# Attention with two-bank maxima, an earlier turn of the maxima, the query copy on VectorE and one transpose of the biases

## The reference, cut to what matters

```python
xn  = layernorm(x)
q, k, v    = split(xn  @ Wqkv     + bqkv)        # 16 heads of 8
_, ka, va  = split(ctx @ Wqkv_aux + bqkv_aux)
p, pa = softmax(q @ k.T / sqrt(8)), softmax(q @ ka.T / sqrt(8))
out   = (p @ v) * (1 - gate) + (pa @ va) * gate
x     = x + tanh(g_xattn) * (out @ Wo + bo)
x     = x + tanh(g_ffn) * moe(layernorm(x))
```

## Time and profile before

| what | value |
|---|---|
| median of three runs | 863.81 us (863.57 to 864.4) |
| the profiled execution, its own time | 864.29 us |
| its span on the core | 861.5 us |
| granted TensorE clock, mean over the span | 1.00 |
| busy share of the span: TensorE, VectorE, ScalarE, GpSimd | 96%, 80%, 66%, 74% |
| instructions | 20208 |

### The profile page before, as it was taken

How to read it: one execution, slowest core, us unless ns; L and a number is a source line. 1 busy time by engine, 2 the same in 40 slices (tenths; PEclk the granted TensorE clock), 3 DMA queues, 4 the chain that set the end, 5 groups by cost and what they waited for, 6 DMA issues and landing times.

```text
span 861.5 us, 20208 instructions
## 1 busy us (share of the span) xinstructions
PE 825.7 (96%) x6739; PEld 632.7 (73%) x6739; DVE 687.3 (80%) x1648; ACT 569.5 (66%) x968; POOL 635.7 (74%) x602
## 2 busy tenths in 40 slices
PE   5699999999999899999999999999999999999997
PEld 3366666666666578888888888878888888888885
DVE  6799899898888769769678887867986967876665
ACT  4388888788878765575566576557567556655553
POOL 2567888878854367877886787777787777788785
PEclk9999999999999999999999999999999999999999
DMA  4677777787662166647545654764754655646552
GB/s 114 167 172 167 167 188 158 175 177 168 153 142 56 52 151 137 152 112 165 135 125 143 138 145 110 158 151 101 158 147 116 161 137 126 154 114 153 135 138 58
DMA packets 107630, 120.02 MB, mean 139 GB/s; under 512 B 28154, under 2 KB 69948, under 8 KB 106092
## 3 DMA queue, kind: packets, MB, share of 16 engines
q1 hardware_dynamic: 104652, 118.23, 57.8%
q10 hardware_dynamic: 2880, 0.59, 0.4%
HBM read 103.55 MB, written 14.71 MB: 137 GB/s over the span
## 4 chain that ended last, share of the span: by engine, by line
PE 82%; DMA 6%; DVE 4%; SPq 3%; issue 2%; ACT 2%; POOL 1%; DVEq 0%; ACTq 0%; POOLq 0%
PE bank L2020 20%; PE bank L2022 20%; PE bank L2021 20%; PE bank L1350 5%; PE bank L1336 4%; PE bank L1305 3%; DMA stack_k<-k_scratch 2%; PE bank L1287 2%; DMA stack_q<-nmaxT 1%; PE bank L1358 1%; DVE mx L1000 1%; SPq L416 1%; SPq L419 1%; PE bank L1371 1%; PE bank L1271 1%
## 5 line engine op out<-in xcount | busy, mean ns | idle before, releaser
L1697 POOL TENSOR_TENSOR hid<-act,cwb 128x512 f32<-128x512 f32 x264 | 422.6, 1611 | 127.6 <-DVE act L1924 64.0
L1750 ACT ACTIVATE silu<-bank 128x512 f32<-128x512 f32 x256 | 152.7, 596 | 185.5 <-PE bank L2022 184.1
L1924 DVE TENSOR_TENSOR act<-silu,bank 128x512 f32<-128x512 f32 (+1 forms) x264 | 180.3, 683 | 112.7 <-ACT silu L1750 76.5
L1932 DVE TENSOR_TENSOR hlo<-hid,hhi 128x512 fp32r<-128x512 f32 x256 | 202.9, 793 | 10.6 <-ACT hhi L1756 10.3
L2020 PE MATMUL bank<-xhi,weights_hi 128*128 128x512 f32 x520 | 206.7, 397 | 0.0
L2022 PE MATMUL bank<-xlo,weights_hi 128*128 128x512 f32 x520 | 204.1, 393 | 0.0
L2021 PE MATMUL bank<-xhi,weights_lo 128*128 128x512 f32 x520 | 203.8, 392 | 0.0
L1756 ACT ACTIVATE hhi<-hid 128x512 fp32r<-128x512 f32 (+1 forms) x264 | 165.1, 626 | 20.7 <-POOL hid L1697 18.6
L1000 DVE TENSOR_REDUCE mx<-bank 128x4 f32<-128x512 f32 x240 | 156.0, 683 | 23.9 <-PE bank L1305 22.6
L795 ACT ACTIVATE prob<-bank 128x1024 f32<-128x1024 f32 x128 | 130.9, 1023 | 42.2 <-PE bank L1336 38.8
L2022 PEld LDWEIGHTS bank<-xlo,weights_hi 128*128 128x128 f32 x520 | 97.5, 188 | 22.0
(11 more groups left out here) (241 smaller groups left out, 991.5 us busy)
## 6 DMA issues: line engine op xcount, KB each, us to landing
cwb<-wts_scratch SPq DMA_DIRECT2D x174, 384.0 KB, 5.4
stack_k<-k_scratch SPq DMA_DIRECT2D x30, 256.0 KB, 4.4
k_scratch<-parts_k SPq DMA_DIRECT2D x15, 384.0 KB, 3.4
stack_q<-q_scratch SPq DMA_DIRECT2D x30, 128.0 KB, 2.9
stack_k<-k_scratch SPq DMA_DIRECT2D x30, 128.0 KB, 5.3
q_scratch<-parts_q SPq DMA_DIRECT2D x15, 192.0 KB, 2.4
xin<-in_x_dram SPq DMA_DIRECT2D x16, 128.0 KB, 2.7
cin<-in_ctx_dram SPq DMA_DIRECT2D x16, 128.0 KB, 2.4
```

What stands on the lines that cost most here:

```text
L1697: pool.tensor_tensor(h_buf[k][:], a_buf[k][:], cwb[slot][:, q % GP, :], ALU.mult).then_inc(h_ok, 1)
L1750: act.activation(s_buf[k % RS][:], g_bank[k % 2][:], ACT.Silu).then_inc(s_ok, 1)
L1924: nc.vector.tensor_tensor(a_buf[k % RS][at], s_buf[k % RS][at], u_bank[k % 3][at], ALU.mult).then_inc(a_ok, 1)
L1932: nc.vector.tensor_tensor(hlo[k % RH][:], h_buf[k % RS][:], hhi[k % RH][:].bitcast(F32), ALU.subtract).then_inc(hl_ok, 1)
```

## The change

The diff, cut to its core; the lines that are left out are the context around it.

```diff
--- before.py
+++ after.py
@@ -226,7 +226,7 @@
     mid_at = m.at
     V = [m(f"V{i}", [P, 2, CH, H, VW], F32) for i in range(2)]
     prob = [m(f"prob{i}", [P, 2, HPU * P], F32) for i in range(RP)]
-    brow, brow_in = (prob[0][0:1, k, 0:3 * P] for k in range(2))
+    brow, brow_in = (prob[0][0:3, k, 0:P] for k in range(2))
     mx = [m(f"mx{i}", [P, 4, HH], F32) for i in range(2)]
     nmax = m("nmax", [P, 8, 2, HH], BF16)
     nmaxT = m("nmaxT", [4 * H, P], BF16)
@@ -379,8 +379,8 @@
 
     def bias_loads(sp):
 
-        sp.dma_start(brow_in[:, 0:2 * P], one(v["bqkv"][0:2 * P])).then_inc(c_in, 16)
-        sp.dma_start(brow_in[:, 2 * P:3 * P], one(v["bqkv_aux"][P:2 * P])).then_inc(c_in, 16)
+        sp.dma_start(brow_in[0:2], v["bqkv"][0:2 * P].rearrange("(o n) -> o n", o=2)).then_inc(c_in, 16)
+        sp.dma_start(brow_in[2:3], one(v["bqkv_aux"][P:2 * P])).then_inc(c_in, 16)
 
     def gate_side(eng, a):
 
@@ -732,10 +732,8 @@
         by_row(wqk[:, 1, :], wqkv[:, 1, :])
         by_row(wqk[:, 2, :], wqkva[:, 1, :])
         act.wait_ge(c_in, 16 * 2)
-        for i in range(3):
-            act.activation(brow[:, i * P:(i + 1) * P].rearrange("a (d f i) -> a d f i", d=DH, f=2),
-                           brow_in[:, i * P:(i + 1) * P].rearrange("a (i f d) -> a d f i", d=DH, f=2),
-                           ACT.Copy).then_inc(b_row, 1)
+        act.activation(brow.rearrange("o (d f i) -> o d f i", d=DH, f=2),
+                       brow_in.rearrange("o (i f d) -> o d f i", d=DH, f=2), ACT.Copy).then_inc(b_row, 1)
 
         def clear_stack_q(i):
             return act.activation(stack_q[i][:].rearrange("p h c t -> p (h c t)").bitcast(F32),
@@ -767,6 +765,7 @@
 
         def copy_k(n):
             wait(act, lo_ok, SPLITS * n)
+            wait(act, q_ev, n + 1)
             act.activation(full_k[:, :, 0, :], misc[0][:, TC:2 * TC].rearrange("p (c t) -> p c t", c=CH),
                            ACT.Identity, bias=bcol[:, 1:2]).then_inc(k_ev, 1)
 
@@ -880,8 +879,6 @@
                         copy_o(b - 1, 1 - odd)
                     if r == (1 if late else 0) and not (last and k == BODY - 1):
                         shift_rows(b + 1)
-                    if odd and r == 0 and n + 3 < NC:
-                        copy_q(n + 3)
                     if first and r == 1:
                         norm(3)
                     if (odd, r) == (0, 3) and more:
@@ -992,21 +989,13 @@
                                               ALU.subtract, ALU.mult)
             ins.then_inc(xn_ok, 1)
 
-        def maxima(b, par, u):
-            wait(dve, s_mm, UNITS * b + u + 1)
-            if u == 0:
+        def joint_maxima(b, r, banks=two_banks):
+            wait(dve, s_mm, UNITS * b + 2 * r + 2)
+            if r == 0:
                 wait(dve, nm_ok, b - 1)
-            f, h = S_ROW[u] // HH, S_ROW[u] % HH
-            nc.vector.tensor_reduce(mx[par][:, 2 * f:2 * f + 2, h:h + 2].rearrange("p a h -> p h a"),
-                                    s_bank[u % 2][:].rearrange("p (h a k) -> p h a k", h=2, a=2),
-                                    AXX, ALU.max).then_inc(mx_ok, 1)
-
-        def first_maxima(b, r):
-            pair = ROUNDS * b + r
-            wait(dve, s_mm, 2 * (pair + 1))
             h = S_ROW[2 * r]
-            nc.vector.tensor_reduce(mx[b][:, :, h:h + 2].rearrange("p (f a) h -> p f h a", f=2),
-                                    (wide, two_banks)[pair % 2][:].rearrange("p (f h a k) -> p f h a k", f=2, h=2, a=2),
+            nc.vector.tensor_reduce(mx[b % 2][:, :, h:h + 2].rearrange("p (f a) h -> p f h a", f=2),
+                                    banks[:].rearrange("p (f h a k) -> p f h a k", f=2, h=2, a=2),
                                     AXX, ALU.max).then_inc(mx_ok, 2)
 
         def minus_max(b, par, turned):
@@ -1023,6 +1012,12 @@
             wait(dve, nm_mm, b + 1)
             wait(dve, shift, 16 * b)
             nc.vector.tensor_copy(nmaxT[:], misc[1][0:4 * H, 0:P // 2].bitcast(BF16)).then_inc(nm_ev, 1)
+
+        def copy_q(n):
+            wait(dve, qk_mm, n + 1)
+            wait(dve, lo_ok, SPLITS * (n - 1) + 1)
+            nc.vector.tensor_scalar(full_q[:], misc[0][:, 0:TC].rearrange("p (c t) -> p c t", c=CH),
+                                    bcol[:, 0:1], None, ALU.add).then_inc(q_ev, 1)
 
         def copy_ka(n):
             wait(dve, ka_mm, n + 1)
@@ -1201,13 +1196,13 @@
         split(1, 1, 1, 0)
         split(1, 1, 1, 1)
         for r in range(ROUNDS):
-            first_maxima(0, r)
+            joint_maxima(0, r, (wide, two_banks)[r % 2])
         minus_max(0, 0, 3)
         norm_sums(3)
         evac_nmax(0)
         norm_mean(3)
         for r in range(ROUNDS):
-            first_maxima(1, r)
+            joint_maxima(1, r, (wide, two_banks)[r % 2])
             if r == 1:
                 copy_ka(2)
         minus_max(1, 1, 3)
@@ -1223,10 +1218,10 @@
                     if u == 0 and b == NB - 2:
                         dve.wait_ge(fe_ok, 1)
                         minus_max(NB - 1, 1, NC)
-                    if two_more:
-                        maxima(b + 2, odd, u)
                     if u == (1 if late else 0) and one_more:
                         evac_nmax(b + 1)
+                    if two_more and u % 2 == 0:
+                        joint_maxima(b + 2, u // 2)
                     if u == 7 and two_more and b + 2 < NB - 1:
                         minus_max(b + 2, odd, min(n + 4, NC))
                     if u == 3 and first:
@@ -1239,7 +1234,9 @@
                         norm_sums(n + 4)
                     if u == 7 and not first:
                         residual(b - 1, *((n, i, 0) if odd else (n - 1, 1 - i, 1)))
-                    if u == 7 and not odd and n + 4 < NC:
+                    if u == 1 and odd and n + 3 < NC:
+                        copy_q(n + 3)
+                    if u == 1 and odd and n + 4 < NC:
                         norm_mean(n + 4)
                     if left == 1 and (k, u) in STATS_AT:
                         first_stats(STATS_AT.index((k, u)))
@@ -1372,12 +1369,8 @@
             nc.tensor.matmul(o, attT[:, 1, :], wo[:, 1, :], start=False, stop=True).then_inc(wo_mm, 1)
 
         def turn_biases():
-            pe.wait_ge(b_row, 3)
-            pe.wait_ge(kones_ok, 4)
-            for i in range(3):
-                ins = nc.tensor.matmul(st_bank[0][:, i:i + 1], brow[:, i * P:(i + 1) * P], ones[0:1, 0:1],
-                                       start=True, stop=True)
-            ins.then_inc(b_mm, 1)
+            pe.wait_ge(b_row, 1)
+            nc.tensor.transpose(st_bank[0][:, 0:3], brow, ident[0:3, 0:3]).then_inc(b_mm, 1)
 
         def turn_max(b):
             wait(pe, nm_ok, b + 1)
@@ -1490,9 +1483,9 @@
                             weighted(b, odd, u - LAG, n, i)
                         elif not first:
                             weighted(b - 1, 1 - odd, u + UNITS - LAG, n if odd else n - 1, i if odd else 1 - i)
-                    if r == 0 and one_more and not late:
-                        wait(pe, nm_ev, b + 1)
-                        turn_max(b + 1)
+                        if u == 0 and one_more and not late:
+                            wait(pe, nm_ev, b + 1)
+                            turn_max(b + 1)
                     if r == 0 and odd and n + 3 < NC:
                         wait(pe, v_ev, n + 2)
                         project_qk(n + 3, 1 - i)
```

## The result

| | before | after |
|---|---|---|
| median | 863.69 us (863.05 to 864.4, 4 runs) | 875.71 us (874.42 to 876.57, 4 runs) |
| ratio | | 1.0138, 95% interval 1.012 to 1.0155 |
| span of the profiled execution | 861.5 us | 872.6 us |
| thirteen chunks, from TensorE's first round on | 38.31 to 245.35, 207.0 us | 38.54 to 256.42, 217.9 us |
| shortest chunk in steady state (the floor) | 15.6 us | 16.26 us |

The kernel is slower by 12.0 us in the medians and 11.1 us in the spans (the execution profiled after, 874.42 us, is the fastest of its four). 10.8 of these 11.1 us lie in the thirteen chunks, 0.2 ahead of the first round, and nothing behind them. The page's chain says that TensorE holds even more of it than in the earlier trace rows; the largest group of VectorE there is now the joint maxima.

The account below looks back on a forecast made before the run. Bound: TensorE's 15.62 us chunk floor plus waits from a tight two-chunk loop from mean to loads. Loop +9.0, first chunk +0.35, start -0.15, last batches -0.4: +8.8, giving 872.5 us (forecast 869 to 877, range 863 to 878).

Parts of the forecast that it names:

- the mean's loop of two chunks: Attention, VectorE's mean through GpSimd's splits to TensorE's stack_k loads: 33.3 us after against 31.8, +9.0 for twelve chunks; chance 0.52.
- The mean moves later: VectorE, odd batches: the mean starts at 97.3 instead of 95.30, 2.0 us later, and GpSimd can't win it back.
- the rival of quicker loads: DMA loads in longer chunks land in 4.4 us, so the loop is 32.5 us and the time 867.5; chance 0.20.
- SP: Rival: SP, late with store_k anyway, absorbs the mean's delay; only even batches' 0.35 us counts, 868 us; chance 0.08.
- Scores that wait for both banks: TensorE, even batches: the next scores wait 0.35 us for the joint maximum (0 to 0.7); odd batches nothing.
- VectorE's work: VectorE: four joint maxima for eight save 0.62 us a batch, 0.78 a chunk after the query copy; counted at nothing.
- The query copy leaves ScalarE: ScalarE, odd batches: second exponential up to 0.47 us sooner, winning TensorE 0 to 0.05 a chunk; taken as 0.
- The shift rows: The DMA of nmaxT starts 0.25 to 0.6 us earlier; late for TensorE only in two chunks, 0.3 and 0.5 us.
- The start: Before the chunks: one bias reordering and matmul instead of three wins about 0.15 us (nothing to 0.75).
- The waits of GpSimd: GpSimd, each chunk: its wait for the mean stays about 1.3 us.
- The last batches: VectorE, about six last rounds: a joint maximum of 1.21 instead of pairs of 1.27 us gives 0.4 us back.

Follow-up runs that it names:

- a_mean_back: The changed kernel with norm_mean(n + 4) back in the even batch, u = 7: 869.46 us, ratio 1.007 to the kernel before.
- b_mean_late: The kernel before with one edit, norm_mean(n + 4) moved to the odd batch, u = 1: 869.52 us, ratio 1.0055.
- b_turn_split: The kernel before with one edit, turn_max between the two units of the sums in round 0: 868.77 us, ratio 1.006.
- b_joint: The kernel before with the joint maxima alone; evacuation behind the first of them, turn, mean and query copy where they were: 872.29 us, ratio 1.0102.
- p_reorder: The kernel before with TensorE's weighted sums first, then turns and projections, no longer between scores and sums: 866.71 us, ratio 1.0031.
- b_copyq: The kernel before with the query copy alone moved from ScalarE to VectorE, in odd batches: 863.46 us, ratio 1.0006.

## Why the prediction was right, and where its sum was not

The sign and the place are right: 875.71 us lies inside the range of 863 to 878, and the likeliest case (the mean's loop of two chunks) is the one that the trace, a_mean_back and b_mean_late show. The time was 3.2 us too low. By its steps:

- **The mean moves later, 2.0 us.** Right. Without the move it starts at 8.9 (a_mean_back), with it at 11.0; turn, evacuation, joint maximum (1.21), query copy (0.48) and mean follow each other in the order and nearly with the times forecast.
- **The loop of two chunks.** Right, and its sum closer than it deserved, by luck. Forecast 33.3 = 10.85 (the mean) + 17.2 + 5.2; measured by the same method over twelve chunks 33.2 = 11.0 + 16.7 (16.0 to 18.4) + 5.5, and two mean chunks are 33.5 (200.89 / 6). The way from the mean to the issue was 0.5 us shorter than forecast, and the landing 0.3 and the mean 0.15 longer, so the errors cancelled. The last load lands in 5.5 us on average, in the kernel before in 5.6, where the forecast took 5.2 from the median of all loads; so the rival of quicker loads is out, and so is SP: with 16.7 us from the mean to the issue, it gave back 0.5 of the 2.0 us.
- **Scores that wait for both banks, 0.35 us in even batches.** This is the step that failed, in its cause. I placed the turn, the evacuation and the joint maximum at 0.97, 1.24 and 1.37 to 2.58 us after the round's start, and the trace has 0.94, 1.20 and 1.34 to 2.55. But I let TensorE come for the bank at its old time. It comes 0.29 us later, because the round has become longer, and finds the bank free or nearly so (0.1 us). What I had not counted is the turn between two sums as an edit to TensorE itself: three changes of tile shape where there was one. It costs 0.29 us in round 0 of even batches and 0.39 in odd ones, in which I had counted nothing. Behind it come 0.07 and 0.11 in rounds 2, and -0.25 in round 1 of odd batches: the second exponential starts 3.09 us after the batch's start, as before (3.10), so of the 0.39 that round 0 takes, round 1 had 0.25 to give. That is 0.64 us a chunk in all, nearly twice the term that I had. The turn alone, in b_turn_split, makes 0.27 and 0.36 in rounds 0 and 0.44 in all; what makes the rest is open.
- **The size.** Of 11.1 us in the spans, 10.84 are in the chunks (forecast 9.35), 0.23 at the start (forecast -0.15) and nothing behind (forecast -0.4). The late mean alone costs 6.1 us (b_mean_late, 869.52 - 863.43), everything but the late mean costs 6.0 (a_mean_back, 869.46 - 863.43), and together they cost 12.0. That this adds up is partly chance, since alone the mean was moved by 1.3 us and in the change by 2.5. The table behind this list fits another reading better: whichever of the loop and the floor is longer sets the pace. In the kernel after it is the loop; with the mean back, the raised floor is left.
- **The sums themselves.** Three of them were slightly off. The last window of the earlier trace rows runs past its chunk by 0.67 us (it has 281 matmuls, not 264), so two chunks took 31.7 us and not 31.8; 873.1 less 0.5 is 872.6; and the rival of quicker loads comes to 867.8.
- **VectorE's work.** The saving of 0.62 us a batch was counted from the mean length of one maximum, but the records of two maxima in a row overlap: a pair takes 1.28 us and not 1.37 (the row at 107.15, under b_joint). VectorE is busy with maxima for 10.42 us of a chunk before and 9.75 after, so 0.33 us a batch were saved. With the query copy its time in a chunk did not fall, as forecast, but rose from 14.2 to 14.4 us. The time of the kernel doesn't hang on this term, which stood in the sum at nothing.
- **The query copy leaves ScalarE.** Counted at 0 to 0.05 us a chunk; alone it gives 0.1 of floor (15.53 against 15.61), and no difference in the median.
- **The shift rows.** Right: two waits of TensorE for the copied maxima, 0.8 us in all before, are gone, and the chunks don't show it.
- **The start.** The first query store goes out at 13.40 instead of 13.61, about as forecast, and the first round still begins at 38.54 instead of 38.31. Over the six kernels with one transpose the first round begins at 37.8 to 38.8 us (mean 38.3), over the eight with three matmuls at 38.3 to 38.8 (mean 38.5). What the bias edit gives is at most 0.2 us, and these runs can't separate it from nothing.
- **The waits of GpSimd.** I wrote that its wait for the mean would stay at 1.3 us. It is 2.5 (30.5 / 12). That was an error of bookkeeping: if its work is the same and the chunk is 0.8 us longer, it must stand 0.8 us longer somewhere.
- **The last batches.** 0.4 us was to come back through a shorter maximum; from the end of the thirteenth chunk to the last round it is 45.0 us against 44.9 before. Why it did not is not settled.

The loop (mean, way to the issue, landing) against the floor, means over the chunks of one profiled execution each. What is measured lies up to 0.3 us above the longer of the two, since the loop varies from chunk to chunk:

| us for two chunks | the loop | two floors | measured |
|---|---|---|---|
| before | 31.4 | 31.2 | 31.7 |
| b_mean_late | 32.4 | 31.1 | 32.7 |
| b_turn_split | 31.1 | 32.1 | 32.2 |
| a_mean_back | 31.5 | 32.5 | 32.5 |
| after | 33.2 | 32.5 | 33.5 |

## What to carry to other kernels

An instruction that is moved "one slot earlier" on TensorE has a price of its own when its tile shape differs from its neighbours': read the gaps ahead of each change of shape in the weight-load rows before moving it, put instructions of one shape next to each other, and count the changes in the new order, since another order can have as many (p_reorder). A joint instruction that saves work on an engine that is not the bound makes each thing behind it wait for the longer one; follow what is queued behind it, through every in-order queue, to the engine that is the bound. And when a loop of several chunks is tight, moving its first member early helps only down to the next member that waits for something else.

## What the runs showed of the hardware

TensorE's weight loads stand idle by nearly the same amount each time where the tile shape changes, and nearly all of these rows name no semaphore: 0.20 us from the 32-column tiles of the sums to the full tile (89.52 and 90.04 above, 108.10 and 108.62 in the kernel after), 0.21 from 48 rows to the 32-column tiles (107.75), 0.06 to 0.08 from a single bf16 turn back to them (89.62 to 89.68). Between equal shapes there is no such gap: 0.31 us of loads at 103.68 follow the turn at 103.67 at once. From the full tile to the 32-column tiles it is 0.17 (105.72), and from the 32-column tiles to 64 rows 0.20 (113.93 in b_copyq). The joint maximum over 1024 columns takes 1.22 us, and two maxima over 512 in a row 1.28 (107.15), since their records overlap, although one by itself takes 0.68: two instructions in one save 0.06 us here, not the 0.15 that twice 683 ns would give.
